# First attention: the inverse sums are multiplied into each head's probabilities on GpSimd, and no longer turned once a group

## What is computed

```python
q = (x @ Wq).reshape(B, N, h, dh).transpose(0, 2, 1, 3) * scale
kv = x @ Wkv
k, v = (kv[..., :dh], kv[..., dh:])
sim = jnp.einsum('bhid,bjd->bhij', q, k)
...
sim = sim + bias.transpose(2, 0, 1)[None] * bias_scale
sim = jnp.where(causal[None, None], -jnp.finfo(sim.dtype).max, sim)
attn = jax.nn.softmax(sim, axis=-1)
out = jnp.einsum('bhij,bjd->bhid', attn, v)
out = out.transpose(0, 2, 1, 3).reshape(B, N, h * dh)
return out @ Wout + bout
```

## Time and profile before

| | |
|---|---|
| median of 3 runs | 1112.66 us |
| lowest and highest of these | 1111.88 and 1114.72 us |
| span of the profiled execution | 1103.5 us |
| TensorE busy | 964.7 us, 87% |
| VectorE busy | 762.6 us, 69% |
| ScalarE busy | 592.7 us, 54% |
| GpSimd busy | 330.1 us, 30% |
| mean granted TensorE clock | 0.927 |

### The profile page before, as it was taken

How to read it: one execution, slowest core, us unless ns; L and a number is a source line. 1 busy time by engine, 2 the same in 40 slices (tenths; PEclk the granted TensorE clock), 3 DMA queues, 4 the chain that set the end, 5 groups by cost and what they waited for, 6 DMA issues and landing times. The chain is left out here.

```text
span 1103.5 us, 18648 instructions
## 1 busy us (share of the span) xinstructions
PE 964.7 (87%) x6220; PEld 628.0 (57%) x6220; DVE 762.6 (69%) x2263; ACT 592.7 (54%) x1165; POOL 330.1 (30%) x417
## 2 busy tenths in 40 slices
PE   6889999999999999999749388689999999997474
PEld 4767666767766776677539344344444444444463
DVE  6767758676677767577623699887888888862523
ACT  4866757666676766567312192315555555564120
POOL 2522122211321111122144209143544344521523
PEclk9999999999999999999759598878999999998577
DMA  6440000000000000000250100000000000000623
GB/s 201 110 125 2 1 1 1 1 1 1 1 1 1 1 1 1 1 2 1 83 168 29 48 1 0 1 1 1 1 2 1 1 2 1 1 1 1 206 59 100
DMA packets 49546, 32.16 MB, mean 29 GB/s; under 512 B 9339, under 2 KB 46124, under 8 KB 49452
## 3 DMA queue, kind: packets, MB, share of 16 engines
q1 hardware_dynamic: 47404, 26.72, 8.7%
q0 software_dynamic: 2048, 4.26, 1.2%
HBM read 21.38 MB, written 11.69 MB: 30 GB/s over the span
## 5 line engine op out<-in xcount | busy, mean ns | idle before, releaser
L562 ACT ACTIVATE attn_a_prob<-attn_a_score,attn_a_m_all 128x128 f32<-128x128 f32 (+7 forms) x256 | 188.8, 740 | 50.9 <-DVE attn_a_m_all L482 47.0
L912 ACT ACTIVATE attn_b_probT<-attn_b_st 128x1024 f32<-128x1024 f32 (+1 forms) x192 | 145.2, 808 | 129.5 <-PE attn_b_st L778 128.2
L478 DVE TENSOR_REDUCE attn_a_m_far<-attn_a_score 128x1 f32<-128x512 f32 (+3 forms) x192 | 105.6, 550 | 78.5 <-PE attn_a_score L390 76.3
L402 PE MATMUL attn_a_slot<-tab,attn_a_prob 128*128 128x128 f32 x1152 | 148.8, 273 | 1.4 <-ACT attn_a_prob L562 1.2
L402 PEld LDWEIGHTS attn_a_slot<-tab,attn_a_prob 128*128 128x128 f32 x1152 | 131.7, 140 | 9.9 <-issue 2.1
L414 PE MATMUL attn_a_o<-attn_a_ptsa,Vd 128*64 128x512 f32 x288 | 136.4, 603 | 0.0
L414 PE MATMUL attn_a_o<-attn_a_ptsb,Vd 128*64 128x512 f32 x288 | 136.4, 603 | 0.0
L841 DVE CUSTOM_DVE_ANT_0 attn_b_slot<-attn_b_slot,later 128x128 f32<-128x128 f32 (+3 forms) x256 | 118.5, 521 | 17.8 <-PE attn_b_slot L753 17.8
L571 ACT ACTIVATE attn_a_ptsa<-attn_a_slot 128x512 f32<-128x512 f32 x144 | 85.8, 596 | 80.6 <-PE attn_a_slot L402 80.0
L753 PE MATMUL attn_b_slot<-KS,attn_b_alone 128*128 128x512 f32 (+2 forms) x384 | 123.8, 417 | 4.1 <-POOL attn_b_alone L934 2.5
L482 DVE CUSTOM_DVE_ANT_0 attn_a_score<-attn_a_score,bias_near,attn_a_m_far 128x256 f32<-128x256 f32 (+2 forms) x192 | 107.4, 559 | 6.8
(11 more groups left out here) (244 smaller groups left out, 1855.8 us busy)
## 6 DMA issues: line engine op xcount, KB each, us to landing
moe_weights_w<-in_L_ffn_w_dram SPq DMA_DIRECT2D x32, 256.0 KB, 5.2
to_experts<-xn SPq DMA_DIRECT2D x2, 1056.0 KB, 11.9
moe_experts_xe<-to_experts SPq DMA_DIRECT2D x16, 132.0 KB, 2.9
bias_by_query_and_key<-bias_by_distance SPq DMA_DIRECT2D x2, 1024.0 KB
bias_near<-bias_by_query_and_key SPq DMA_DIRECT2D x2, 1024.0 KB, 6.4
from_experts<-xn SPq DMA_DIRECT2D x2, 1024.0 KB, 11.7
moe_experts_back<-from_experts SPq DMA_DIRECT2D x8, 256.0 KB, 3.8
X<-in_L_attn_a_x_dram SPq DMA_DIRECT2D x2, 512.0 KB, 4.7
```

What stands on the lines that cost most here:

```text
L402: ins = nc.tensor.transpose(dst[:, jj * P:(jj + 1) * P], probs(g)[:, 2 * jj + half, i * P:(i + 1) * P], ident[:, :])
L478: nc.vector.tensor_reduce(least, score[t % 2][:, at:at + nk - win], AX.X, ALU.min).then_inc(far_done, 1)
L562: nc.scalar.activation(probs(g)[:, j, 0:nk], score[t % 2][:, at:at + nk], ACT.Exp, bias=m_all[:, j:j + 1], scale=-1.0, accum_out=rowsum[g ...
L912: nc.scalar.activation(probT[n % 2][:, two, lo:], st[:, two, lo:], ACT.Exp, scale=-1.0).then_inc(exp_done, 1)
```

## The change

The exponentials are divided where they stand. VectorE takes the reciprocals in pairs of heads, at every second tick, one tick behind their exponentials (`invert(g, pair)`). GpSimd multiplies each head's probabilities by its inverse in place (`weigh`). The widening, the four transposes and the copy to `R` are gone, and with them `RAT`; VectorE now only copies `o` to `OT` (`keep_sums`). TensorE's first turning of a group waits for all eight multiplications instead of all eight exponentials, and `steps_at` spreads the steps over the ticks 2 to 7 instead of 1 to 7. On GpSimd the two halves of the query differences stand behind the multiplications of heads 3 and 5, and the copies between groups come at other groups.

```diff
-        return [i for i in range(steps(g)) if 1 + i * (HS - 1) // steps(g) == j]
+        return [i for i in range(steps(g)) if 2 + i * (HS - 2) // steps(g) == j]
...
                 if i == 0:
-                    pe.wait_ge(exp_done, (g + 1) * HS)
+                    pe.wait_ge(weighed, (g + 1) * HS)
...
-            def spread_inverse(g):
-
-                dst = open_slot(slot["r", g])
-                pe.wait_ge(widened, g + 1)
-                for jj in range(BLK):
-                    ins = nc.tensor.transpose(dst[:, jj * P:(jj + 1) * P],
-                                              wide[g % 2][:, jj * P:(jj + 1) * P], ident[:, :])
-                ins.then_inc(slot_filled, 1)
...
-            def invert(g):
-
-                dve.wait_ge(exp_done, (g + 1) * HS)
+            def invert(g, pair):
+
+                two = slice(2 * pair, 2 * pair + 2)
+                dve.wait_ge(exp_done, g * HS + 2 * pair + 2)
                 if g >= 2:
-                    dve.wait_ge(widened, g - 1)
-                nc.vector.reciprocal(rinv[g % 2][:, :], rowsum[g % 2][:, :]).then_inc(inverted, 1)
-
-            def scale_sums(g):
+                    dve.wait_ge(weighed, (g - 2) * HS + 2 * pair + 2)
+                nc.vector.reciprocal(rinv[g % 2][:, two], rowsum[g % 2][:, two]).then_inc(inverted, 1)
+
+            def keep_sums(g):
 
                 dve.wait_ge(summed, steps_before[g + 1])
-                dve.wait_ge(spread, g + 1)
...
-                nc.vector.tensor_tensor(OT[g % 2][:, :], o_ps[:, :], R[g % 2][:, :], ALU.mult).then_inc(scaled, 1)
+                nc.vector.tensor_copy(OT[g % 2][:, :], o_ps[:, :]).then_inc(scaled, 1)
...
                 if j == 0 and g >= 2:
-                    scale_sums(g - 2)
+                    keep_sums(g - 2)
                 if 0 < g <= GROUPS:
                     for i in steps_at(g - 1, j):
                         move(g - 1, i)
-                    if j == 1:
-                        invert(g - 1)
+                if j % 2 == 0 and 0 < g * HS + j <= UNITS:
+                    invert((g * HS + j - 2) // HS, (j - 2) % HS // 2)
...
+            def weigh(g, j):
+
+                pool.wait_ge(inverted, (g * HS + j) // 2 + 1)
+                p = probs(g)[:, j, 0:P * steps(g)]
+                nc.gpsimd.tensor_scalar(p, p, rinv[g % 2][:, j:j + 1], None, ALU.mult).then_inc(weighed, 1)
...
             for g in range(GROUPS):
-                widen(g)
-                if g + 2 < GROUPS:
-                    pool.wait_ge(widened, g + 1)
-                    split_queries(g + 2)
+                for j in range(HS):
+                    weigh(g, j)
+                    if g + 1 < GROUPS and j in (3, 5):
+                        pool.wait_ge(weighed, g * HS + j + 1)
+                        split_queries(g + 1, j // 2 - 1)
+                        pool.wait_ge(queries_ready, 2 * g + j // 2)
+                pool.wait_ge(weighed, (g + 1) * HS)
                 if g == 0:
+                    copies(pool, "bias", 0)
+                if g == 2:
                     copies(pool, "weights")
```

## The result

The changed kernel takes 1292.27 us (median of 4 runs, 1290.12 to 1294.22), the kernel before 1112.62 us (4 runs, 1111.88 to 1114.72). The ratio is 1.164, with an interval from 1.162 to 1.166: 180 us slower. The forecast was 50 us slower, and its range ended at 1212.

The account below looks back on a forecast made before the run. The prediction took TensorE as the bound in the first attention. Its terms, -11 + 53 + 0 + 8 = +50 us on a span of 1103.5, plus 9.2 for the runs' median, gave 1162 us, range 1129 to 1212.

Parts of the forecast that it names:

- What bounds the kernel before: First attention: TensorE, busy 496.2 of 520 us, is the bound; nearly every microsecond it loses lengthens the program.
- What is taken away (-11): TensorE loses 128 transposes of the widened inverse, 0.35 us for each of 32 groups: 11.2 us less.
- Off the path (0): VectorE's 128 reciprocals of two columns instead of 32 of eight: 18 us more work, under its 155 us idle.
- The 256 multiplications (237 us): GpSimd's multiplications of all heads, each 0.42 us + 0.00088 x columns, 237 us together.
- the high end: Upper estimate: multiplications at the two-input slope, stalls of 89 us, some 20 clock falls: +112 us, 1225.
- second rival: GpSimd's multiplications near the two-input slope, long-group stalls of 4 to 5 us: 1190 to 1225 us; chance 0.22.
- Both signs: Wrong in size if GpSimd's new row grows 2 ns a column or the stage's clock is 0.50 over 30 us.
- The stalls (+53): TensorE waits before turning each group for GpSimd's last two heads: 14.4 + 59 - 20 = 53 us.
- the formula: One stall before turning is 0.45 + 2W - S: W one GpSimd multiplication, S one head's scores on TensorE.
- +4 us, at the start alone: GpSimd's output bias before the second group's multiplications delays query differences TensorE needs: +4 us, between 0 and 6.
- The clock (+8): Five stalls exceed 2 us and drop TensorE's clock to half, 1.7 us lost each: +8 us, ends 0 and 25.
- third rival: TensorE's clock falls after most stalls: 32 x 1.7 = 54 us instead of 8, giving 1209 us; chance 0.10.

Follow-up runs that it names:

- e1: The changed kernel without GpSimd's 256 multiplications, the probabilities staying undivided; the first turning waits for the reciprocals instead: 1101.6 us.
- e2: The changed kernel with each multiplication over the first 128 keys only, all waits and the order kept: 1155.2 us.
- e4: The changed kernel with both halves of the query differences behind head 3's multiplication instead of behind heads 3 and 5: 1301.6 us.
- e9: The changed kernel with turning in ticks 4 to 7 and both halves of the query differences behind head 3: 1197.9 us.
- e5: The changed kernel with turning spread over ticks 4 to 7 instead of 2 to 7, nothing else: 1203.6 us.
- e3: The changed kernel with idle transposes of the identity on TensorE ahead of its waits for multiplications and query differences, to hold the clock: 1278.2 us.
- e12: The changed kernel with turning in ticks 4 to 7 and the query differences' halves behind heads 1 and 3, all multiplications on GpSimd: 1182.4 us.
- e7: The changed kernel with all 256 multiplications on VectorE, each pair behind its reciprocal; GpSimd keeps the query differences: 1174.2 us.
- e6: The changed kernel with heads 6 and 7 of each group multiplied on VectorE behind their reciprocal, heads 0 to 5 on GpSimd: 1211.6 us.

## Why the prediction was wrong

**What bounds the kernel before:** right. TensorE was the bound, and time that it lost lengthened the program.

**What is taken away (-11):** right in sign, too large. e1 leaves the multiplications out and gains 6.5 us. Its TensorE work falls by 12 us and its stage by 7: TensorE is idle for 26 us instead of 21. The waits for exponentials stayed (16.2 us, 16.8 before); new are 3.2 us for inverses and 2.9 for ScalarE's copies of slot a.

**Off the path (0):** right. The 128 reciprocals take 20.1 us at 157 ns instead of 192, the copy of the sums 691 ns as foreseen, and e1, which has them all, isn't slower.

**The 256 multiplications (237 us): the step that failed.** "I take the copies' slope, as the operation has one wide input" put 0.88 ns on a column; it is 2.50, more than even the two-input operations' 2.13 of the high end. From this came "GpSimd then works about 320 of 520 us, so it isn't the bound in sum". It works 523 us, and the stage before was 515. e2 takes most of the columns away and 135 of the 180 us with them; e1 takes all. The record at 128 columns could have warned: there the tensor-scalar took 531 ns against 455 for two inputs, as the prediction noted under its second rival, and still gave that rival 0.22 and only the two-input slope. Its 1190 to 1225 was the nearest case, and too low by 67 us at its end. Both signs that the prediction gave for being wrong in size came: a row that grows at 2 ns a column or more, and over 30 us at 0.50. The estimate from the Trainium skill (GPSIMD Engine Reference, section 3.1), 1.5 ns a column, was nearer but too low as well; the trace decides for 2.50.

**The stalls (+53):** the place and the formula were right, the rest was not. There is a wait before the turning in 31 of 32 groups, by GpSimd, as said. With the measured W the formula gives 14 + 110 - 20 = 105 us, and 78.2 were found. The whole sum would then have been -11 + 105 + 8 = +102, some 78 us short of the 180, so the price of a column isn't all. The second step that failed is the wait for the query differences, which the prediction put at +4 us, at the start alone. They hold TensorE in 32 places for 75.8 us, because their second half stands behind the multiplications of heads 4 and 5 and those wait for an inverse in their turn. e4 shows that this wait feeds the other: taken away, it came back before the turning in full, and in e9 against e5 in part (32 us less of it, 20 more there). The other way round it doesn't hold: in e5 the turning's wait goes, and the scores' wait doesn't grow (66.4 instead of 75.8). How long this wait is with the W assumed (0.53 to 1.32 us) was not tried; e2 with W = 0.6 at every length still has 12.7 us of it, and by the prediction's terms (33 of stalls less 11) it should have lost 22 us to the kernel before, where it lost 47.

**The clock (+8):** too small as a count. Instead of five falls there are 29 stretches with 151 us at 0.50. The third rival priced such falls at 54 us over all stalls; e3 took 113 us at half away and won 12, net of its own overlong filling. So the clock's price lies between 12 us and, as an estimate, the 56 us that TensorE is busy beyond e1 (538.7 against 482.3). That rival assumed that TensorE's time is the program's; in the long groups of e3 only 11 us of at most 33 came back, or 19 if all that the filling took there was on the path. How much the other 38 us cost was not tried.

**What made it 180.** Without multiplications 1101.6 us; with multiplications of 0.6 us 1155.2, which is the price of waiting for even short ones; with their true length 1292.3. The last 135 us or so are read as a ring: scores make exponentials, these make inverses, GpSimd multiplies and then lets TensorE go on to scores. At 523 us GpSimd has no slack for its own waits. e12, with the same work in a better order, loses 74 us to the kernel before instead of 180. Its stage of 586 us is 71 longer than the 515 of before: GpSimd's work alone is 9 more than those 515, and the other 62 are GpSimd's idle time, 43 of it waits for inverses. Whether an order exists that takes these away too was not tried.

## What to carry to other kernels

Before work goes to an engine that looks idle, sum that work at the price of the same operation at the size used; if only another size is on record, take the dearest slope in the trace as the likely one, not the cheapest (here even the dearest was too low). Compare the sum with the length that the stage has before the change: at 523 us of work in 515 there is no room for any wait, and at 238 (e2) the waits that cross between two engines already cost 54 us against e1. When one wait in such a ring is taken away, look where it turns up before counting the gain.

## What was not expected of the hardware

GpSimd multiplies by a per-partition scalar at 2.50 ns a column, slower than its own two-input operations (2.13) and nearly three times its copies (0.88).

VectorE does the same multiplication much faster, but slows where GpSimd is at work at the same moment. In e7 the median is 286 ns at 128 columns and 751 at 1024, 0.52 ns a column; the longest took 2718. The groups by line and shape, of e7 and then of e6:

```profile
L484 DVE TENSOR_SCALAR attn_a_prob<-attn_a_prob,attn_a_rinv 128x1024 f32<-128x1024 f32 x32 | 26.0, 855 | 0.6
```

```profile
L488 DVE TENSOR_SCALAR attn_a_prob<-attn_a_prob,attn_a_rinv 128x1024 f32<-128x1024 f32 x8 | 10.3, 1334 | 0.1
```

Of e7's 32 of 1024 columns, the 28 that overlap no instruction of GpSimd took at most 755 ns; the four that overlap a query difference took 1366 to 1683. One of these four is the first of the two here (147.70 to 149.35):

```profile
147.53 1.27 POOL L580 TENSOR_TENSOR QS_0b<-raw,QS_0b 64x512 fp32r<-64x512 f32 x1 [1.35 <-ACT QS_0b L537]
147.70 2.32 DVE L484 TENSOR_SCALAR attn_a_prob<-attn_a_prob,attn_a_rinv 128x1024 f32<-128x1024 f32 x2
```

In e6 all eight of 1024 columns overlap a multiplication or a query difference of GpSimd, and their median is 1441. GpSimd's own 1024 columns take 2844 ns in e6 too, but its query differences stretch there as well: ten of the 17 that overlap a multiplication of VectorE took 1440 to 1787 ns, the others at most 1290. The Trainium skill (SBUF — State Buffer, section "Who interferes with whom") says that the two engines share a pair of ports which the first to come holds for its whole instruction, and names tensor-scalar among the operations of VectorE that may ask for it; these numbers agree, though no run here took the sharing away by itself.

With waits of 2 to 5 us between dense work the granted clock was 0.50 in 29 separate stretches of this stage, where the waits of up to 1.7 us before left it at 1.00. Holding it up gave back 12 us net, and in the long groups 11 of at most 33, where GpSimd set the pace in part.
